# One token block per pass: the slot matmuls moved ahead of the transposes, the gate activations waiting for two products instead of three

## The reference

```python
xn = _layernorm(x, axis=-1)
# branch 1: a gated scan over the tokens
w, k, u = xn @ Wp[:, :1024] + bp0, xn @ Wp[:, 1024:2048] + bp1, xn @ Wu + bu
gate = sigmoid(w_t)
s = gate * (s * tanh(k_t) + u_t) + (1 - gate) * s        # over t
branch1 = ys @ Wo + bo
# branch 2: 64 slots
h = gelu(ctx @ w1 + b1)
route_logits = (h @ w2 + b2) / (abs(tau) + 0.1)
alpha = softmax over the 8 largest of 64 logits, else 0
slot_input = alpha.T @ xn;  denom = alpha.sum(tokens)
# slot_input / denom goes through a GRU cell, an attention over slots, a layer norm and wvp
branch2 = (alpha @ slot_values) @ wo + bo
out = x + branch1 + branch2
```

## Time and profile before

| what | us |
|---|---|
| median of 2 runs | 1912.64 |
| the two runs | 1902.32, 1922.97 |
| the profiled execution, its own time | 1899.89 |
| its span on the slowest core (core 4) | 1898.3 |
| spans of the eight cores | 1877.4 to 1898.3 |

### The profile page before, as it was taken

The page is one execution under the profiler, slowest core; times in us unless marked ns, Lnnn a source line. Parts: engine busy times, 40 slices in busy tenths (PEclk is TensorE's granted clock), DMA queues, the critical chain, the costliest instruction groups (busy, mean ns, idle before and its releaser), DMA issues.

```text
span 1898.3 us, 20757 instructions; the slowest of 8 cores (1877.4 to 1898.3 us)
## 1 busy us (share of the span) xinstructions
PE 1525.8 (80%) x7085; PEld 674.3 (36%) x7221; DVE 748.7 (39%) x1359; ACT 568.6 (30%) x926; POOL 27.0 (1%) x54
## 2 busy tenths in 40 slices
PE   0098989889898898989889898998944359899997
PEld 0043434444343443434434343443411123333332
DVE  0145546364453635546354463635520202222222
ACT  0252524334252352524434153352200211211110
POOL 0100000000000000000000000000011000000000
PEclk9999989899899999999899898999966669999898
DMA  9632020220202102020120202101069545565555
GB/s 151 131 57 89 1 89 13 77 90 1 89 1 89 59 31 89 1 89 22 68 89 1 89 1 89 60 30 45 1 136 167 102 100 189 199 208 191 183 194 199
DMA packets 42679, 166.52 MB, mean 88 GB/s; under 512 B 4290, under 2 KB 5458, under 8 KB 41682
## 3 DMA queue, kind: packets, MB, share of 16 engines
q1 hardware_dynamic: 36178, 134.29, 20.3%
q0 software_dynamic: 6400, 30.89, 10.0%
HBM read 128.68 MB, written 67.11 MB: 103 GB/s over the span
## 4 chain that ended last, share of the span: by engine, by line
PE 68%; DMA 10%; DVE 9%; issue 6%; ACT 3%; DVEq 3%; ACTq 0%; SPq 0%; POOL 0%; POOLq 0%
PE psA L1038 7%; PE psA L441 6%; PE psA L437 6%; PE psC L446 6%; PE psB L446 6%; PE psC L441 6%; PE psB L437 6%; PE psA L507 4%; PE psA L299 3%; PE psB L507 3%; PE psB L1038 3%; PE psC L1038 3%; DMA sb_bq_c<-bq_pk 2%; DVEq L102 2%; DMA sb_WT<-Wih_pk 2%
## 5 line engine op out<-in xcount | busy, mean ns | idle before, releaser
L477 DVE SCALAR_TENSOR_TENSOR sb_a_sb<-sb_g_sb,sb_s_sb 128x512 f32<-128x512 f32 x128 | 88.6, 692 | 341.3 <-ACT sb_s_sb L462 341.3
L19 ACT ACT_TABLE_LOAD x83 | 106.5, 1283 | 351.2 <-PE psA L507 347.4
L489 DVE TENSOR_TENSOR_SCAN sb_ys_bf<-sb_a_sb,sb_ys_bf,sb_b_sb 128x512 bf16<-128x512 f32 x120 | 154.0, 1283 | 9.0
L437 PE MATMUL psA<-sb_xn_f,sb_Wp_sb 128*128 128x512 bf16 x448 | 126.2, 408 | 35.2 <-DVE sb_alpha_T L377 32.5
L1038 PE MATMUL psA<-sb_wo_sb,sb_z_f 128*128 128x512 bf16 x504 | 135.3, 429 | 23.6 <-ACT sb_z_f L1007 21.2
L1053 DVE TENSOR_TENSOR sb_prd<-psA,sb_prd 128x1024 f32<-128x1024 f32 x32 | 39.2, 1225 | 272.7 <-DMA sb_prd<-out 188.4
L299 PE MATMUL psA<-sb_Wo_sb,sb_ys_bf 128*128 128x512 bf16 x480 | 118.3, 383 | 29.2 <-DVE sb_x_sl L327 27.5
L441 PE MATMUL psA<-sb_xn_f,sb_Wp_sb 128*128 128x512 bf16 x512 | 129.9, 400 | 0.0
L460 ACT ACTIVATE sb_g_sb<-psA,sb_bpw 128x512 f32<-128x512 f32 x64 | 44.0, 687 | 271.1 <-PE psB L446 267.2
L441 PE MATMUL psC<-sb_xn_f,sb_Wp_sb 128*128 128x512 bf16 x512 | 121.0, 379 | 0.0
L446 PE MATMUL psB<-sb_xn_f,sb_Wu_sb 128*128 128x512 bf16 x512 | 121.0, 379 | 0.0
(11 more groups left out here) (224 smaller groups left out, 1888.9 us busy)
## 6 DMA issues: line engine op xcount, KB each, us to landing
sb_x_sl<-x SPq DMA_DIRECT2D x32, 1024.0 KB, 7.0
out<-sb_x_sl SPq DMA_DIRECT2D x32, 1024.0 KB, 4.9
sb_prd<-out SPq DMA_DIRECT2D x16, 2048.0 KB, 11.6
out<-sb_prd SPq DMA_DIRECT2D x32, 1024.0 KB, 4.8
sb_WT<-Wih_pk POOLq DMA_DIRECT2D x12, 512.0 KB, 8.7
sb_whh_pp<-Whh_pk POOLq DMA_DIRECT2D x12, 512.0 KB, 8.5
sb_Wp_sb<-Wp_pk POOLq DMA_DIRECT2D x1, 4096.0 KB, 34.0
sb_Wu_sb<-Wu_pk POOLq DMA_DIRECT2D x1, 2048.0 KB, 38.1
```

The lines of the kernel that those rows point to most:

```text
L19: return eng.add_instruction(mybir.InstLoadActFuncSet(name=eng.bass.get_next_instruction_name(), act_func_set_id=idx, ins=[], outs=[]))
L437: P.op("pe", lambda e, j=j, k=k, psw=psw: e.matmul(psw, t.Wp_sb[:, k, j * 128:(j + 1) * 128], t.xn_f[:, k, :], start=(k == 0), stop=(k == ...
L477: P.op("ve", lambda v, pp=pp: v.scalar_tensor_tensor(t.a_sb[:], t.g_sb[:, pp, :], -2.0, t.s2_sb[:, pp, :], ALU.mult, ALU.mult))
L489: P.op("ve", lambda v, j=j, init=init: v.tensor_tensor_scan(t.ys_bf[:, j, :], t.a_sb[:], t.b_sb[:], init, ALU.mult, ALU.add), inc="sve", e ...
```

## The change

In each round, `slot_pe(ph-1)` and `slot_ve(ph-1)` now stand right behind `wo_block(ph-1)`, ahead of the transposes, and no longer between the logits and `wku_loop`. The last k matmul of each `j` now also signals (event "wk"); ACT's sigmoids wait for it and no longer for the last u matmul ("wku"), for which DVE now waits itself. In `h_logits` the pipeline drain ahead of each Gelu is gone, and the logits of the first tile wait for the four Gelus one at a time and no longer for the last one before they start.

```diff
@@ wku_loop @@
             for k in range(ND):
+                last = (k == ND - 1)
                 P.op("pe", lambda e, j=j, k=k, psk=psk: e.matmul(
                     psk, t.Wp_sb[:, k, 1024 + j * 128:1024 + (j + 1) * 128],
-                    t.xn_f[:, k, :], start=(k == 0), stop=(k == ND - 1)))
+                    t.xn_f[:, k, :], start=(k == 0), stop=(k == ND - 1)),
+                    inc="spe" if last else None,
+                    event=("wk", ph, j) if last else None)
...
-            P.wait("se", ("wku", ph, j))
+            P.wait("se", ("wk", ph, j))
...
             P.wait("ve", ("gs", ph, j))
+            P.wait("ve", ("wku", ph, j))
@@ h_logits @@
-            P.drain("se")
             P.op("se", lambda s, jh=jh, ps=ps: s.activation(
                 t.h_f[:, jh, :], ps, AF.Gelu, bias=t.bias_h[:, jh:jh + 1]),
...
-        P.wait("pe", ("hf", ph, NH - 1))
         pe_claim("C0")
         for i in range(TPT):
             for kh in range(NH):
+                if i == 0:
+                    P.wait("pe", ("hf", ph, kh))
@@ the loop over the rounds @@
-        if ph < NPH:
-            xn_transposes(ph)
-            h_logits(ph)
         if ph >= 1:
             slot_pe(ph - 1)
             slot_ve(ph - 1)
         if ph < NPH:
+            xn_transposes(ph)
+            h_logits(ph)
             wku_loop(ph)
```

## The result

The kernel after took 1814.9 us (median of 11 runs) beside 1902.2 for the kernel before (median of 10). The ratio is 0.954 with a 95% interval of 0.950 to 0.957: 4.6% faster. Forecast were 1821 us and a gain of 79.9 us; the two profiled executions, 1899.9 and 1811.8 us, lie 88.1 us apart.

A forecast was written before the change was run, and what follows sets the result against it. PE was taken to set the pace of the first pass, through its waits and clock. Terms 22.9 + 37.7 + 4.3 + 20.2 - 6.8 + 1.6 = 79.9 us, off 1899.9, gave 1820.0, stated as 1821 us; range 1800 to 1848.

The forecast's parts named there:

- Step 1: Block end: gates waiting for k alone start DVE's chain 1.43 us earlier, 16 blocks, 22.9 us gained.
- Step 2: Slot matmuls ahead of transposes: 5.34 us a block removed, 2.83 added, 37.7 us gained; plus 4.3 from two low-clock blocks.
- step 5: Logits: three matmuls move under the wait for the fourth Gelu, drains find ACT idle; 1.6 us gained together.
- Step 3: Start of `wku_loop`: nearly all w matmuls begin at full clock, 12 x 1.68 = 20.2 us gained.
- Step 4: Gelu product: all 15 start at low clock, lasting a little deeper, 9.05 us each; cost 6.8 us.
- B: Block end: something other than the gates holds DVE's chain, so step 1's gain is lost; 1844 us, chance 0.08.
- C: Transposes: late T1 makes them run one group at a time, 67 us worse; 1888 us, chance 0.04.
- D: From Gelu product into `wku_loop`: low clock lasts on after the longer sparse stretch, slower; 1926 us, chance 0.03.

The follow-up runs named there:

- e4: The kernel after with the gate edit taken back, new order and logit edits kept: 1837.3 us, ratio 0.965 to the kernel before.
- e5: The kernel after with each block's first w matmul also waiting for DVE's maxima: 1871.0 us, ratio 0.985 to the kernel before.
- e8: The kernel after with each block's first w matmul also waiting for ACT's copy of the logits: 1816.8 us, ratio 0.960 to the kernel before.
- e1: The kernel before with only the gate edit (ACT waits for k, DVE for u): 1872.1 us, ratio 0.983.
- e2: The kernel before with only the slot matmuls and DVE's slot work moved ahead of the transposes: 1845.2 us, ratio 0.970.
- e7: The kernel after with slot matmuls in portions between the transposes and DVE's slot work behind the copies: 1747.8 us, ratio 0.922 to the kernel before.
- e6: The kernel after with DVE copying alpha out first and adding the slot sums behind the eight copies: 1783.1 us, ratio 0.940 to the kernel before.
- e9: The kernel before with only the drains ahead of the Gelus removed: ratio 1.000 (0.998 to 1.001).

## Why the prediction was right, step by step

- **Step 1, the gates:** right in mechanism and size. 1.45 us earlier on DVE in the trace (forecast 1.43), 0.32 us left of PE's wait (0.33), 22.4 us by e4 (22.9). One block too many was counted: the wait for L327 stands in 15 blocks, and in the last round of the kernel before tile 3 starts without idle time, so 15 x 1.43 = 21.5.
- **Step 2, the order:** right in mechanism, some 0.35 us a block too good ahead of the Gelu product. From the slot matmuls' start to that product I had 8.72 us; blocks whose transposes keep full clock take 2.20 + 6.53 = 8.73, but the mean is 9.02, since in 90 of 120 blocks the low clock reaches the transposes. Behind the Gelu product 5.73 us a block went (8.19 to 2.46, means), and 5.34 + 0.1 (step 5) + 4.3/15 = 5.73 had been counted.
- **Step 3, the clock of the w matmuls:** right in size, 1.20 us a block (the whole of `wku_loop`, 42.59 to 41.39, means), 18 us where 20.2 were forecast for core 4. The reason given was too easy: e5 shows that 2.1 us of waiting there bring the low clock back in nearly every block, e8 that 1.2 us did not at its even spacing.
- **Step 4, the Gelu product's clock:** wrong in sign. "I expect none to escape and a low clock a little deeper": forecast +0.45 us a block (-6.8 us in the sum). Measured -0.43 (8.51 to 8.08), +6.4 us. I had treated the lot of a block as fixed by the length of the sparse stretch; e8, with a stretch as long and 111 of 120 products at full clock, shows that the length does not fix it. That its place in time does is the likeliest reading and not shown by itself. The page's rule that I set beside this step (the Trainium skill, TensorE: Matmul & The Clock Gate, HAM oscillation — how this bites in real kernels) would have made it 15 of 15 blocks; on core 3 it is 12. The page tells of an array that waits for DMA between K-tiles; here it works part of the time.
- **Step 5, small edits:** mis-sized. The split wait is worth 0.23 us a block, 3.5 us, not 1.6; PE's wait fell by 4.5 us in the kernel after (18.0 to 13.5). The drains cost nothing, as forecast.

Together, in the first pass and as means over the eight cores: 84.3 us measured, 78.5 forecast (79.9 less the sixteenth 1.43 of step 1, which would lie behind it). Of the 5.8 us between them step 4 is 13; the low clock in the transposes takes 5 back, step 3 another 2. Step 5's surplus adds nothing, as the whole stretch behind the Gelu product came out as counted. So the total came closer than its parts: an error of 13 us in step 4 stood against 7 us of errors the other way, and that is luck. Rivals B and C fell with e1 and with the boundary's timeline (T1 comes late once, 1.60 us, and the groups then go in pairs). D did not come near: in the kernel after the clock was back at full over the last 0.5 us of every product.

## What to carry to other kernels

Ask of every small group of matmuls what it waits for and who waits for its answer, and place it where both are idle anyway: moved from the one place to the other the slot matmuls gave 3% (e2). Spread through PE's gaps between the transposes, with DVE's share behind the copies, they gave 3.4% more (e7 beside the kernel after); nearly half of that came already with DVE's share alone (e6). A wait of PE ahead of dense matmuls is to be priced twice, once as idle time and once as the low clock that may follow. When a signal can come from the last product that is read rather than from the last one issued, the whole chain behind it moves, and its worth is what remains at its far end.

## What the runs showed of the hardware that I had not expected

- A wait of 1.2 us ahead of the w matmuls left their clock at 1.00 in 14.6 of 15 blocks (e8, evenly spaced blocks); one of 2.1 us made it 0.50 to 0.70 in 14.6 of 15 (e5).
- 18 us of added waiting cost nothing in the first pass (e8): the Gelu products ran at full clock in 111 of 120 blocks, 6.91 us instead of up to 9.8, behind the same sparse stretch that went with a low clock in 90 of 120 blocks of the kernel after.
- Explicit drains ahead of an activation on an idle ACT: 64 of them, no cost that a measurement to 0.12% shows (e9).
